# One round's down projection, scatter, residual add and store in two halves: an adaLN and routed-FFN kernel on one Trainium2 core

## The reference

```python
# conditioning: gates, a causal moving average with modulated inputs, layer norm
h = L0_cond_ref(x, ...)                       # (128, 32, 128)

# routed feed-forward: per batch, the 16 best-scored tokens of 32
scores = jnp.einsum('bsd,d->bs', h, w_router)
top_scores, top_idx = jax.lax.top_k(scores, 16)
weights = jax.nn.sigmoid(top_scores)
selected = jnp.take_along_axis(h, top_idx[:, :, None], axis=1)
g = jax.nn.gelu(jnp.einsum('bkd,df->bkf', selected, W1) + b1)      # up: 128 -> 512
processed = jnp.einsum('bkf,fd->bkd', g, W2) + b2                  # down: 512 -> 128
update = weights[:, :, None] * processed
y = x + h.at[top_idx].add(update)             # scatter and residual
```

## Time and profile before

| | us |
|---|---|
| three runs: median | 182.54 |
| lowest, highest | 182.26, 183.22 |
| span of the profiled execution, first to last instruction | 180.8 |
| median less that span | 1.74 |
| PE busy in the span | 169.3 (94%) |
| DVE busy | 131.8 (73%) |
| POOL busy | 130.9 (72%) |
| ACT busy | 93.9 (52%) |

### The profile page before, as it was taken

One profiled execution on the slowest core, in us unless ns is written; L12 is line 12 of the kernel. 1 busy time (PEld: TensorE's weight loads), 2 busy tenths in 40 slices (PEclk: granted clock), 3 DMA queues, 4 the chain that ended last, 5 costly groups with the idle time before them and its releaser, 6 DMA issues.

```text
span 180.8 us, 3266 instructions
## 1 busy us (share of the span) xinstructions
PE 169.3 (94%) x1122; PEld 128.1 (71%) x1122; DVE 131.8 (73%) x197; ACT 93.9 (52%) x160; POOL 130.9 (72%) x137
## 2 busy tenths in 40 slices
PE   5699999999999999999999999999999999999960
PEld 4594458875566778587579687579669869888860
DVE  1536799989887898946968886987868549968122
ACT  2246997436257253835281248356483767593600
POOL 7547604895948979888969989939994894299920
PEclk9999999999999999999999999999999999999997
DMA  4797000000000000000000000000000040040404
GB/s 119 170 257 187 4 0 0 0 2 4 0 2 0 4 0 0 4 0 0 0 0 4 0 2 0 4 0 0 2 4 0 2 115 5 0 120 0 116 0 116
DMA packets 12751, 5.60 MB, mean 31 GB/s; under 512 B 2848, under 2 KB 12608, under 8 KB 12736
## 3 DMA queue, kind: packets, MB, share of 16 engines
q1 hardware_dynamic: 11872, 5.20, 10.9%
q10 hardware_dynamic: 864, 0.20, 0.5%
HBM read 3.30 MB, written 2.10 MB: 30 GB/s over the span
## 4 chain that ended last, share of the span: by engine, by line
PE 70%; DVE 8%; issue 7%; POOL 6%; ACT 4%; DMA 2%; ACTq 1%; POOLq 0%; DVEq 0%
PE ring L1060 25%; PE ring L1044 4%; PE ring L1017 4%; PE ring L1122 4%; PE ring L996 4%; PE ring L1018 4%; PE ring L1033 4%; DVE ring L780 2%; DMA prod<-in_L_cond_Wsoma_dram 2%; PE ring L1106 2%; PE ring L1075 2%; PE ring L1067 2%; PE ring L1050 2%; POOL small L481 2%; PE ring L1024 2%
## 5 line engine op out<-in xcount | busy, mean ns | idle before, releaser
L469 POOL TENSOR_TENSOR ctx_acc<-ctx_acc,prod 128x832 f32<-128x832 f32 (+14 forms) x60 | 78.6, 1321 | 27.3 <-DVE prod L825 23.6
L825 DVE TENSOR_TENSOR prod<-ring,gm 128x832 f32<-128x832 f32 (+14 forms) x60 | 40.0, 686 | 10.7 <-PE ring L1060 9.0
L1060 PE MATMUL ring<-mod_hi,decayed_lo 128*128 128x320 f32 (+11 forms) x96 | 31.3, 380 | 0.8 <-DVE mod_nat L801 0.4
L1060 PE MATMUL ring<-mod_hi,decayed_hi 128*128 128x320 f32 (+11 forms) x96 | 27.0, 335 | 0.0
L1060 PE MATMUL ring<-mod_lo,decayed_hi 128*128 128x320 f32 (+11 forms) x96 | 26.9, 335 | 0.0
L1060 PEld LDWEIGHTS ring<-mod_hi,decayed_lo 128*128 128x128 f32 x96 | 16.5, 189 | 11.7 <-issue 7.8
L812 DVE TENSOR_TENSOR state<-ring,blend_w 128x1024 f32<-128x1024 f32 x16 | 18.8, 1218 | 1.0 <-PE ring L1033 0.9
L1060 PEld LDWEIGHTS ring<-mod_lo,decayed_hi 128*128 128x128 f32 x96 | 17.6, 189 | 1.3 <-issue 0.4
L1060 PEld LDWEIGHTS ring<-mod_hi,decayed_hi 128*128 128x128 f32 x96 | 17.6, 189 | 1.0
L1122 PE MATMUL ring<-w_sb,gm 128*128 128x128 f32 x128 | 15.0, 275 | 0.0
L1122 PEld LDWEIGHTS ring<-w_sb,gm 128*128 128x128 f32 x128 | 14.6, 192 | 0.0
(11 more groups left out here) (170 smaller groups left out, 333.5 us busy)
## 6 DMA issues: line engine op xcount, KB each, us to landing
x_nat<-in_x_dram SPq DMA_DIRECT2D x4, 512.0 KB, 4.8
out_dram<-x_nat SPq DMA_DIRECT2D x4, 512.0 KB, 3.2
w_sb<-in_L_ffn_W_dram SPq DMA_DIRECT2D x2, 256.0 KB, 4.5
down<-in_cond_dram SPq DMA_DIRECT2D x2, 64.0 KB, 4.1
prod<-in_L_cond_Wg_dram ACTq DMA_DIRECT2D x1, 128.0 KB, 3.8
prod<-in_L_cond_Wsoma_dram ACTq DMA_DIRECT2D x1, 64.0 KB, 4.4
bn<-in_L_cond_bn_dram SPq DMA_DIRECT2D x4, 0.1 KB, 3.3
down<-in_L_cond_Wtemp_dram SPq DMA_DIRECT2D x1, 64.0 KB, 4.2
```

The lines of the kernel that those rows point to most:

```text
L469: nc.gpsimd.tensor_tensor(dst, dst, packed(prod[:, n % NP, 0:width(r)], r, k), ALU.add).then_inc(acc_done, 1)
L825: nc.vector.tensor_tensor(dst, packed(slot(step), r, k), lagged(gated(r), r, k), ALU.mult).then_inc(read(step), 1)
L1060: last = nc.tensor.matmul(to[:, c], w[:, k, :], src[:, c], start=(i == 0), stop=(i == len(parts) - 1))
```

## The change

A new table `PARTS` gives the number of parts in which a round does its last steps: one for rounds 0 to 2, two for round 3. For round 3

- `down` becomes `down:3.0` (pairs 0 and 1) and `down:3.1` (pairs 2 and 3), each of eight matmuls into a bank of its own, each with its own waits for `up:3.0` and `up:3.1`, and each with its own DVE instruction of 128x256;
- `scatter` becomes `scatter:3.0` and `scatter:3.1`, each of four matmuls into two banks of its own, each with its own DVE add of 128x512;
- the store becomes two DMAs of four tiles (256 KB) each, each behind its own half's add. SP's final wait counts five stores in place of four.

In the list the word `residual:3` now stands ahead of `down:3.0`; it is POOL's step, and POOL has none of the others, so its order stays.

```diff
+PARTS = (1, 1, 1, 2)
...
-turn_pick:2 pick:3 down:2 gather:3 scatter:2 up:3.0 up:3.1 plus_beta:3 turn_pick:3 down:3 residual:3
-scatter:3
+turn_pick:2 pick:3 down:2 gather:3 scatter:2 up:3.0 up:3.1 plus_beta:3 turn_pick:3 residual:3
+down:3.0 down:3.1 scatter:3.0 scatter:3.1
...
+        def pairs_of(r, k):
+            n = tiles(r) // 2 // PARTS[r]
+            return range(k * n, (k + 1) * n)
+        def places(buf, r, k):
+            n = tiles(r) // PARTS[r]
+            return tiles_of(buf, r)[:, k * n:(k + 1) * n]
...
             for r in range(R):
-                step = ("scatter", r, 0)
-                sp.wait_ge(read(step), reads_after(step))
-                sp.dma_start(tiles_of(y_dram, r), tiles_of(x_nat, r)).then_inc(y_out, 16)
-            sp.wait_ge(y_out, R * 16)
+                for k in range(PARTS[r]):
+                    step = ("scatter", r, k)
+                    sp.wait_ge(read(step), reads_after(step))
+                    sp.dma_start(places(y_dram, r, k), places(x_nat, r, k)).then_inc(y_out, 16)
+            sp.wait_ge(y_out, sum(PARTS) * 16)
...
                 elif kind == "down":
...
-                    n = tiles(r) // 2
+                    at = pairs_of(r, k)
+                    n = len(at)
                     nc.vector.tensor_tensor(
-                        down[:, 0:n, :], slot(step)[:, 0:n * E].rearrange("p (n e) -> p n e", e=E),
+                        down[:, at.start:at.stop, :], slot(step)[:, 0:n * E].rearrange("p (n e) -> p n e", e=E),
                         b2_r[:, None, :].to_broadcast([P, n, E]), ALU.add).then_inc(read(step), 1)
                 elif kind == "scatter":
                     dve.wait_ge(res_done, r + 1)
-                    n = tiles(r) // 2
-                    res = tiles_of(x_nat, r).rearrange("p (n h) e -> p h n e", h=2)
+                    n = len(pairs_of(r, k))
+                    res = places(x_nat, r, k).rearrange("p (n h) e -> p h n e", h=2)
...
                     for i in UPS[r]:
                         pe.wait_ge(read(("up", r, i)), reads_after(("up", r, i)))
                         for f in (2 * i, 2 * i + 1):
-                            for n in range(tiles(r) // 2):
+                            pairs = pairs_of(r, k)
+                            for n in pairs:
...
                 elif kind == "scatter":
-                    pe.wait_ge(read(("down", r, 0)), reads_after(("down", r, 0)))
+                    pe.wait_ge(read(("down", r, k)), reads_after(("down", r, k)))
                     pe.wait_ge(read(("turn_pick", r, 0)), reads_after(("turn_pick", r, 0)))
-                    for n in range(tiles(r)):
-                        rows = slice(n % 2 * SEL, (n % 2 + 1) * SEL)
+                    pairs = pairs_of(r, k)
+                    for n in pairs:
+                        for h in range(2):
+                            rows = slice(h * SEL, (h + 1) * SEL)
```

More of the change, by code:

```diff
@@ L666, in _ @@
                     if r:
-                        last = ("scatter", r - 1, 0)
+                        last = ("scatter", r - 1, PARTS[r - 1] - 1)
                         act.wait_ge(full(last), filled(last))
@@ L912, in _ @@
                 elif kind == "down":
-                    if r == 0:
+                    if (r, k) == (0, 0):
                         dve.wait_ge(ffn_in, 4 * 16)
-                    n = tiles(r) // 2
+                    at = pairs_of(r, k)
+                    n = len(at)
                     nc.vector.tensor_tensor(
-                        down[:, 0:n, :], slot(step)[:, 0:n * E].rearrange("p (n e) -> p n e", e=E),
+                        down[:, at.start:at.stop, :], slot(step)[:, 0:n * E].rearrange("p (n e) -> p n e", e=E),
                         b2_r[:, None, :].to_broadcast([P, n, E]), ALU.add).then_inc(read(step), 1)
@@ L1116, in _ @@
                         for f in (2 * i, 2 * i + 1):
-                            for n in range(tiles(r) // 2):
+                            pairs = pairs_of(r, k)
+                            for n in pairs:
                                 at = f * tiles(r) * SEL + n * P
-                                first = f == 2 * UPS[r][0] and n == 0
-                                final = f == 2 * UPS[r][1] + 1 and n == tiles(r) // 2 - 1
-                                last = nc.tensor.matmul(dst[:, n * E:(n + 1) * E], inner(r, at, at + P), w2_sb[:, f, :],
+                                to = dst[:, (n - pairs.start) * E:(n - pairs.start + 1) * E]
+                                first = f == 2 * UPS[r][0] and n == pairs.start
+                                final = f == 2 * UPS[r][1] + 1 and n == pairs.stop - 1
+                                last = nc.tensor.matmul(to, inner(r, at, at + P), w2_sb[:, f, :],
                                                         start=first, stop=final)
                 elif kind == "scatter":
-                    pe.wait_ge(read(("down", r, 0)), reads_after(("down", r, 0)))
+                    pe.wait_ge(read(("down", r, k)), reads_after(("down", r, k)))
                     pe.wait_ge(read(("turn_pick", r, 0)), reads_after(("turn_pick", r, 0)))
-                    for n in range(tiles(r)):
-                        rows = slice(n % 2 * SEL, (n % 2 + 1) * SEL)
-                        at = n % 2 * BANK + n // 2 * E
-                        last = nc.tensor.matmul(dst[:, at:at + E], pick_t[rows, n // 2, :], down[rows, n // 2, :],
-                                                start=True, stop=True)
+                    pairs = pairs_of(r, k)
+                    for n in pairs:
+                        for h in range(2):
+                            rows = slice(h * SEL, (h + 1) * SEL)
+                            at = h * BANK + (n - pairs.start) * E
+                            last = nc.tensor.matmul(dst[:, at:at + E], pick_t[rows, n, :], down[rows, n, :],
+                                                    start=True, stop=True)
                 last.then_inc(full(step), 1)
```

## The result

The changed kernel took 180.97 us (median of 4 runs, 180.03 to 181.44), the kernel before 182.88 us beside it (4 runs, 182.26 to 183.36). The ratio is 0.989, 95% interval 0.985 to 0.993: about 1.1% faster. A second measurement of both, further down, gave 0.989 again (0.986 to 0.992).

The account below looks back on a forecast made before the run. From 173.73 us on, latency was taken to set the end. The last add 0.78 us earlier and the store 0.90 shorter take 1.68 off the span, giving 179.12; plus 1.74 for the median, forecast 180.9 us, range 180.2 to 181.9.

Parts of the forecast that it names:

- part 1: Round 3's `down` in halves on PE: a new stall of 0.49 us (0.27 to 0.52) waiting for the GELU behind 8 records.
- No stall: Rival on PE's wait in `down`: GELU's end reaches PE in 0.03, 0.22 us comes back, 180.6 us; no chance of its own.
- part 2: Evictions of `down` on DVE: two of 0.42 us for one of 0.69, the first beside PE's work; the second ends 0.23 late.
- part 3: Round 3's scatter and adds in halves: scatter parts and adds 0.69 us each, the last add ending 0.78 us earlier.
- part 4: Round 3's store in halves: each lands after 2.3 us instead of 3.2, the last landing 1.68 us earlier than before.
- a store that doesn't shrink: Rival on round 3's store: a half still takes 3.2 us, gain only 0.78, 181.8 us; chance of landing over 3.0: 0.08.
- stores one after the other at full price: Rival on round 3's stores: the second waits for the first's landing, 184.0 us at 3.2 each; chance 0.05, 0.03 of it slower.
- the halves did overlap: Answers a rival on DVE and PE: halves don't overlap, a stall of about 1.3 us cancels the gain; chance 0.06, 0.01 slower.
- the granted clock: PE's clock, expected to stay at its upper level (1.00); below 1.00 before the last matmul was a sign against the forecast.

Follow-up runs that it names:

- the lone half: Changed kernel without the first half's store of round 3, so the last 256 KB travel alone: span 178.2 us, 8.80 from `down`'s first weight load to the end.
- the single store: Changed kernel with one 512 KB store for round 3 behind the second add: ratio 0.991 to the kernel before, 9.80 us from `down`'s first weight load to the end.

## Why the prediction was right

The sign, the size and the place were right: forecast 180.9 us, measured 180.97; a tail shorter by 1.68, measured 1.73. But five sizes in between were off, some early and some late, and they cancelled; that the tail came out within 0.1 us is luck. So is the time: the kernel before took 182.88 us beside it and not 182.54, so the gain in time was 1.91 where 1.68 was forecast. The mechanism named for the computation held, the one for the store only in part.

| step, in us into the tail | forecast | measured |
|---|---|---|
| PE goes on behind the stall | 1.39 | 1.19 |
| `down:3.1` ends | 4.35 | 4.14 |
| first scatter load | 4.07 | 4.07 |
| second eviction ends | 4.81 | 4.59 |
| first add starts | 4.91 | 4.83 |
| second scatter load | 5.06 | 4.67 |
| first store issued | 5.63 | 5.55 |
| second store issued | 6.54 | 6.18 |
| second store lands | 8.84 | 8.75 |

(Forecast times less 169.88, measured ones less 170.21.)

- **The stall (part 1)** was there, behind the eight records named, by the GELU named, and it was proved by taking away the coarse wait. Its size was 0.29 and not 0.49, inside the range given (0.27 to 0.52): the hand-over from ACT took 0.05. I had taken the 0.25 of PE's waits for DVE, with 0.03 as the other bound, and the truth lay near the other bound. This is nearly the rival "No stall": its hand-over came true, and the 0.2 us that it gave back went in the change of rows, below.
- **The evictions (part 2)**: 0.42 each, the first hidden, as forecast.
- **The scatter (part 3)**: the change from 128-row to 64-row weights costs 0.21, and wasn't in the sum; it ate what the shorter stall had given back. The second hand-over, 0.08 in place of 0.25, and the adds in a row, 1.32 in place of 2 x 0.69 with a pause, brought the second add to its end 0.36 early.
- **The store (part 4)**: 2.3 us for 256 KB was right by itself (the lone half), but the rule that the last landing is the second issue + 2.3 failed: it was 2.6 behind that issue. It needs issues 0.9 apart, and I had them at 0.91, so that the halves "hardly meet". They came 0.63 apart, met, and 0.3 of the 0.36 gained ahead was lost behind the first half's data. The rule with both branches gives the measured end of every run with two stores to within 0.1.
- **The rivals**: a store that doesn't shrink was ruled out by the single store (1.12 and not 1.73) and by the lone half; stores one after the other at full price, by the stretches without a seam; the halves did overlap, and the granted clock was 1.00 until PE had ended.

Of the 1.73 us, the runs attribute 1.12 to the computation in halves with a single store, and 0.61 to splitting the store. Splitting only the add and the store gives 0.60, so the halves of `down`, its eviction and `scatter` bring the other 1.13. The difference of the medians, 1.91, is larger than the tail's; the rest, 0.2, is within the spread of the runs.

## What to carry to other kernels

At the end of a kernel, where each step waits for the whole of the one before, cut the last steps in halves, and with them the store: what counts is when the first store is issued, as long as the next ones arrive before its data is through. Look at the waits when you cut: one that was covered by eight matmuls isn't covered by four, and a wait for each piece cost nothing here. More parts pay as long as the queue can issue them as fast as they become ready: with four stores in place of two, the first was issued 0.5 us earlier, but SP needed 0.42 to 0.54 us from one issue to the next, and 0.2 of the 0.5 was lost. So set the time of an issue beside the time of a part before you choose their number.

## What the hardware showed that I had not expected

- Stores issued from one queue 0.60 to 0.76 us apart form one stream at about 290 GB/s: first issue to the end of the span 3.6 us, as for a single store of the same bytes. A lone 256 KB store takes 2.3 us to land, 512 KB 3.2; four of 128 KB in a row took 2.0 in the median and moved about 250 GB/s.
- SP issued those four stores 0.42, 0.51 and 0.54 us apart, the issues themselves 0.37 to 0.49 us long, and the last one came 0.38 us after its data was ready.
- PE's first weight load of 64 rows behind a block of 128-row loads starts 0.32 us behind the one before, and 0.12 if it has 128 rows too.
- PE's hand-over from another engine was 0.05 to 0.08 us in some places and 0.22 to 0.25 in others, and neither the number of rows nor the length of the idle time ahead explains all of them.
